# A self-attention's row maxima passed on by halves of a group's queries in place of whole groups

## The reference

```
q = q.reshape(B, NUM_KV, GROUPS, N, HEAD_DIM); k, v: [B, NUM_KV, N, HEAD_DIM]
scores = jnp.einsum('bghnd,bhsd->bghns', q, k)
attn = jax.nn.softmax(scores / SCALE, axis=-1)
out = jnp.einsum('bghns,bhsd->bghnd', attn, v)
```

## Time and profile before

| | |
|---|---|
| three runs, median (range) | 1895.57 us (1892.76 to 1900.6) |
| the profiled execution, its time | 1891.45 us |
| its span, from the first to the last instruction | 1889.7 us |
| PE busy | 1787.9 us (95%) |
| DVE busy | 1266.1 us (67%) |
| ACT busy | 1036.9 us (55%) |
| POOL busy | 363.0 us (19%) |
| maxima of pass A, L497 | 1024 times, mean 684 ns |
| exponentials of pass B, L528 | 512 times, mean 1025 ns |

### The profile page before, as it was taken

One profiled execution on the slowest core, in us unless ns is written; L12 is line 12 of the kernel. 1 busy time (PEld: TensorE's weight loads), 2 busy tenths in 40 slices (PEclk: granted clock), 3 DMA queues, 4 the chain that ended last, 5 costly groups with the idle time before them and its releaser, 6 DMA issues. The chain is left out here.

```text
span 1889.7 us, 36142 instructions
## 1 busy us (share of the span) xinstructions
PE 1787.9 (95%) x12036; PEld 1187.4 (63%) x12037; DVE 1266.1 (67%) x2510; ACT 1036.9 (55%) x2238; POOL 363.0 (19%) x403
## 2 busy tenths in 40 slices
PE   6889999999999999988989999997899999999998
PEld 3443333333333333366978899996698888888887
DVE  6588999999999999133248899994757322222323
ACT  2305878888887888921228888885226333333332
POOL 3000000000000000040004222221030444555440
PEclk9956999999999999988899999998999999999999
DMA  5601122111112210045210212111615233333333
GB/s 181 185 10 27 29 39 39 31 28 28 28 28 39 39 30 3 3 119 161 93 54 16 87 32 85 32 31 62 215 58 163 50 50 50 50 50 51 52 56 126
DMA packets 95151, 118.63 MB, mean 63 GB/s; under 512 B 18844, under 2 KB 76624, under 8 KB 93968
## 3 DMA queue, kind: packets, MB, share of 16 engines
q1 hardware_dynamic: 80016, 97.56, 18.7%
q0 software_dynamic: 13920, 19.15, 6.4%
q10 hardware_dynamic: 1104, 0.43, 0.1%
HBM read 70.37 MB, written 41.48 MB: 59 GB/s over the span
## 5 line engine op out<-in xcount | busy, mean ns | idle before, releaser
L497 DVE TENSOR_REDUCE half_max<-psA 128x1 f32<-128x512 f32 x1024 | 634.3, 684 | 36.8 <-PE psA L547 36.4
L528 ACT ACTIVATE PT<-psB 128x1024 f32<-128x1024 f32 x512 | 517.6, 1025 | 164.7 <-PE psB L557 164.5
L547 PE MATMUL psA<-KS,QS 48*128 48x512 f32 x1024 | 407.1, 481 | 23.4 <-PEq L102 14.0
L557 PE MATMUL psB<-QS,KS 50*128 50x512 f32 x1024 | 364.0, 458 | 0.4 <-ACT PT L528 0.4
L576 PE MATMUL psO<-PT,VG 128*32 128x256 f32 x4096 | 329.3, 394 | 4.7 <-ACT OU L518 0.8
L547 PEld LDWEIGHTS psA<-KS,QS 48*128 48x128 f32 x1024 | 168.9, 195 | 247.6 <-DVE half_max L497 188.9
L1866 DVE TENSOR_TENSOR m_silu<-m_psU,m_silu 128x512 f32<-128x512 f32 x104 | 71.8, 691 | 216.4 <-PE m_psU L1694 216.4
L576 PEld LDWEIGHTS psO<-PT,VG 128*32 128x32 f32 x4096 | 82.2, 108 | 191.0 <-issue 120.8
L1347 ACT ACTIVATE x_probs<-x_scores,x_neg_max 128x77 f32<-128x77 f32 x512 | 176.3, 358 | 2.9 <-DVE x_neg_max L1253 2.8
L557 PEld LDWEIGHTS psB<-QS,KS 50*128 50x128 f32 x1024 | 145.1, 187 | 19.9 <-ACT PT L528 17.4
L1197 PE MATMUL psYx<-VO,x_ET 128*128 (+1 forms) x640 | 146.0, 383 | 1.4 <-ACT x_ET L1370 0.9
(11 more groups left out here) (208 smaller groups left out, 2737.7 us busy)
## 6 DMA issues: line engine op xcount, KB each, us to landing
QS<-q_parts SPq DMA_DIRECT2D x96, 128.0 KB
q_parts<-part SPq DMA_DIRECT2D x16, 512.0 KB, 2.7
OT<-OU SPq DMA_DIRECT2D x32, 256.0 KB, 2.6
KS<-k_parts SPq DMA_DIRECT2D x32, 128.0 KB
xf_rows<-XF SPq DMA_DIRECT2D x32, 128.0 KB, 1.7
acc<-X SPq DMA_DIRECT2D x32, 128.0 KB, 1.8
m_x<-xf_rows SPq DMA_DIRECT2D x32, 128.0 KB, 2.1
WG<-in_Wg SPq DMA_DIRECT2D x8, 512.0 KB, 4.1
```

Source lines behind the costliest of these rows:

```text
L497: dve.tensor_reduce(half_max[:, h * TB + t, n:n + 1], psA[:, bank_of(slot, 2 * v + r), :], axis=AX.X, op=ALU.max).then_inc(max_taken, 1)
L528: act.activation(PT[:, k % 4, 2 * a:2 * a + 2, :].rearrange("p h n -> p (h n)"), psB[:, u % 2, :, :].rearrange("p a n -> p (a n)"), ACT.Ex ...
L547: pe.matmul(psA[:, bank_of(slot, m), :], QS[top:top + KQ, slot, h // 2, t * P:(t + 1) * P], KS[top:top + KQ, slot, n * HALF:(n + 1) * HALF ...
L557: mm = pe.matmul(psB[:, u % 2, r, :], KS[top:top + KM, slot, c * P:(c + 1) * P], QS[top:top + KM, slot, a, half * HALF:(half + 1) * HALF], ...
```

## The change

The maxima are handled by halves of a group's queries: 16 steps of pass A are one half. half_max, neg_max, max_parts and max_parts_t are half as wide. VectorE reduces and negates after 16 steps (now L509) and turns five steps into the next half; GpSimd splits twice a group. Both parts of a half now stand in one block of 32 columns, so one store carries them, where a group had two. SyncE does two trips a group, each of one store and two loads of half the row length, before it issues the load of group i+2. TensorE waits for the rows of the first half at step 0 of pass B and for those of the second at step 16; the semaphores rows_set are by half, no longer by even and odd groups. Pass A runs 16 + 10 = 26 steps ahead. The semaphores' counts change with that. The diff, cut:

```diff
@@ -369,10 +369,10 @@
-        half_max = sb("half_max", [P, NU, 2])
-        neg_max = sb("neg_max", [P, NU])
-        max_parts = sb("max_parts", [P, 2, NU], F32R)
-        max_parts_t = sb("max_parts_t", [P, 2, NU])
+        half_max = sb("half_max", [P, NC, 2])
+        neg_max = sb("neg_max", [P, NC])
+        max_parts = sb("max_parts", [P, 2, NC], F32R)
+        max_parts_t = sb("max_parts_t", [P, 2 * NC])
...
-        rows_set = [sem("rows_set_even"), sem("rows_set_odd")]
+        rows_set = [sem("rows_set_first"), sem("rows_set_second")]
...
-            def rows(i, slot):
-
-                sp.wait_ge(mt_done, count(i, 1, 1))
-                for part in range(2):
-                    sp.dma_start(m_parts[i, part, :].rearrange("(u k n) -> k u n", k=4, n=32),
-                                 max_parts_t[:, part, :]).then_inc(m_stored, 16)
-
-                sp.wait_ge(m_stored, count(i, 32, 32))
+            def rows(i, slot, half):
+
+                sp.wait_ge(mt_done, 2 * i + half + 1)
+                sp.dma_start(m_parts[i, half, :].rearrange("(u k n) -> k u n", k=4, n=32), max_parts_t[:, :]).then_inc(m_stored, 16)
+
+                sp.wait_ge(m_stored, 16 * (2 * i + half + 1))
                 for r in range(2):
-                    sp.dma_start(QS.bitcast(F32)[r * ROWS + KQ:r * ROWS + KM, slot, :, :],
-                                 m_parts[i, :, :].rearrange("j (a r n) -> r j a n", r=2, n=S)[r]).then_inc(rows_set[slot % 2], 16)
+                    sp.dma_start(QS.bitcast(F32)[r * ROWS + KQ:r * ROWS + KM, slot, :, half * HALF:(half + 1) * HALF],
+                                 m_parts[i, half, :].rearrange("(j a r n) -> r j a n", j=2, r=2, n=HALF)[r]).then_inc(rows_set[half], 16)
 
             for i in range(NG):
-                rows(i, i % SLOTS)
+                for half in range(2):
+                    rows(i, i % SLOTS, half)
                 if i + 2 < NG:
                     load(i + 2, (i + 2) % SLOTS)
-            for e in range(2):
-                sp.wait_ge(rows_set[e], NROWS * (NG // 2))
+            for half in range(2):
+                sp.wait_ge(rows_set[half], NROWS * NG)
...
-            def maxima(i):
-                pool.wait_ge(v_copied, count(i, 1, 1))
-                pool.wait_ge(neg_done, count(i, 1, 1))
-                if not (isinstance(i, int) and i < 1):
-
-                    pool.wait_ge(mt_done, count(i, 1, 0))
+            def maxima(g):
+                pool.wait_ge(v_copied, g // 2 + 1)
+                pool.wait_ge(neg_done, g + 1)
+                if g:
+
+                    pool.wait_ge(mt_done, g)
                     pool.sem_inc(T["waited_pool"], 1)
                 pool.tensor_copy(max_parts[:, 0, :], neg_max[:, :]).then_inc(m1_done, 1)
-                pool.wait_ge(m1_done, count(i, 1, 1))
+                pool.wait_ge(m1_done, g + 1)
                 pool.tensor_tensor(max_parts[:, 1, :], neg_max[:, :], max_parts[:, 0, :], ALU.subtract).then_inc(m2_done, 1)
-                pool.wait_ge(m2_done, count(i, 1, 1))
+                pool.wait_ge(m2_done, g + 1)
 
             for i in range(NG):
                 values(i, i % 2)
-                maxima(i)
+                for half in range(2):
+                    maxima(2 * i + half)
...
-            def turn_parts(i):
-
-                dve.wait_ge(m2_done, count(i, 1, 1))
-                if not (isinstance(i, int) and i < 1):
-
-                    dve.wait_ge(m_stored, count(i, 32, 0))
-                dve.transpose(max_parts_t[:, :, :], max_parts.bitcast(F32)[:, :, :]).then_inc(mt_done, 1)
-
-            def maxima(i, slot):
-                if not (isinstance(i, int) and i < 1):
-
-                    dve.wait_ge(neg_done, count(i, 1, 0))
-                for v in range(NU):
+            def turn_parts(g):
+
+                dve.wait_ge(m2_done, g + 1)
+                if g:
+
+                    dve.wait_ge(m_stored, 16 * g)
+                dve.transpose(max_parts_t[:, :], max_parts.bitcast(F32)[:, :, :].rearrange("p j u -> p (j u)")).then_inc(mt_done, 1)
+
+            def maxima(i, slot, half):
+
+                g = 2 * i + half
+                if g:
+
+                    dve.wait_ge(neg_done, g)
+                for v in range(half * NC, (half + 1) * NC):
                     for r in range(2):
                         h, t, n = unit_a(v, r)
                         dve.wait_ge(a_done, count(i, 2 * NU, 2 * v + r + 1))
-                        dve.tensor_reduce(half_max[:, h * TB + t, n:n + 1], psA[:, bank_of(slot, 2 * v + r), :],
+                        dve.tensor_reduce(half_max[:, h * (TB // 2) + t % (TB // 2), n:n + 1], psA[:, bank_of(slot, 2 * v + r), :],
                                           axis=AX.X, op=ALU.max).then_inc(max_taken, 1)
-                    if v == TURN_AT and not (isinstance(i, int) and i < 1):
-
-                        turn_parts(count(i, 1, -1))
-
-                dve.wait_ge(max_taken, count(i, 2 * NU, 2 * NU))
-                if not (isinstance(i, int) and i < 1):
-
-                    dve.wait_ge(m2_done, count(i, 1, 0))
+                    if v == half * NC + TURN_AT and g:
+
+                        turn_parts(g - 1)
+
+                dve.wait_ge(max_taken, count(i, 2 * NU, 2 * NC * (half + 1)))
+                if g:
+
+                    dve.wait_ge(m2_done, g)
                 dve.tensor_reduce(neg_max[:, :], half_max[:, :, :], axis=AX.X, op=ALU.max, negate=True).then_inc(neg_done, 1)
 
             for i in range(NG):
-                maxima(i, i % SLOTS)
-            turn_parts(NG - 1)
+                for half in range(2):
+                    maxima(i, i % SLOTS, half)
+            turn_parts(2 * NG - 1)
...
-                pe.wait_ge(rows_set[e], count(i - e, NROWS // 2, NROWS))
                 for u in range(NU):
-                    ahead = 1 if u < NU - LEAD else 2
-                    has_a = not isinstance(i, int) or i + ahead < NG
-                    if u == NU - LEAD and has_a:
-
-                        pe.wait_ge(loaded[e], count(i - e, NLOAD // 2, 2 * NLOAD))
+                    if u % NC == 0:
+                        pe.wait_ge(rows_set[u // NC], NROWS * (i + 1))
+                    ahead = 0 if u < NU - NC - LEAD else 1
+                    has_a = i + ahead < NG
+                    if u == NU - NC - LEAD and has_a:
+
+                        pe.wait_ge(loaded[1 - e], NLOAD * ((i + 1) // 2 + 1))
                     for r in range(2):
                         if has_a:
-                            pass_a(i + ahead, (slot + ahead) % SLOTS, (u + LEAD) % NU, r)
+                            pass_a(i + ahead, (slot + ahead) % SLOTS, (u + NC + LEAD) % NU, r)
                         pass_b(i, slot, u, 1 - r, r == 0)
 
                     if u >= LAG:
                         times_values(i, e, u - LAG)
-                    elif not (isinstance(i, int) and i < 1):
+                    elif i:
                         times_values(i - 1, 1 - e, u - LAG + NU)
 
             pe.wait_ge(loaded[0], NLOAD)
-            for v in range(NU):
+            for v in range(NC + LEAD):
                 for r in range(2):
                     pass_a(0, 0, v, r)
-            pe.wait_ge(loaded[1], NLOAD)
-            for v in range(LEAD):
-                for r in range(2):
-                    pass_a(1, 1, v, r)
             for i in range(NG):
                 group(i, i % SLOTS)
             for u in range(NU, NU + LAG):
...
-        T["m_parts"] = dram("m_parts", [NG, 2, GH * S], F32)
+        T["m_parts"] = dram("m_parts", [NG, 2, 2 * GH * HALF], F32)
```

## The result

The changed kernel takes 1872.78 us, the median of four runs (1866.78 to 1878.54), against 1895.69 us for the kernel before: a ratio of 0.9876, 95% interval 0.9842 to 0.9910. The forecast was 1873.7 us. The profiled execution took 1867.76 us, its span 1866.0.

What follows compares the result with a forecast made beforehand. VectorE and TensorE were nearly always busy in the full-clock common loop, with single-pass ends outside it. Start -19.8, loop +20.3, drain -16.6, boundaries -5.8 make -21.9 us: 1895.57 to 1873.7 us, range 1865 to 1886.

Steps and rivals of the forecast that it cites:

- the clock: Common loop's half-clock stretch stays 19.5 us, so it cancels; rival, rise at another distance: 1868.6 to 1881.8 us, chance 0.12.
- the start: Before pass B: it begins after 26 steps of pass A, not 42, with a shorter first trip; -19.8 us.
- the boundaries: Full-clock loop: 29 boundaries where 14 were, each trip 0.58 us shorter; 2.9 us where 8.7 were, -5.8 us.
- The loop and the drain: Common loop runs one more half, +20.3 us; pass B's drain at the end one half less, -16.6 us.
- The first rival: Trip of the maxima gets no shorter, 29 waits of 0.46 us stay: 1886.4 us, chance 0.09.
- VectorE's new work: 16 more negated maxima and turns, covered: 0 us; rival, VectorE late at every half: +7.6 us, 1881.3, chance 0.07.
- The waits for VectorE: TensorE's three waits in the common loop, 1.2 us, put down to the slots' wrap every four groups; they stay.
- The load in the way of the next trip: SyncE's group load delays the next first-half trip: a loss from 1.6 us each, up to 1962 us; chance 0.04.
- The chances: Whole kernel against a bound of 1886.1 us: 0.87 faster, 0.09 within, 0.04 slower.
- the tenth: Part of the forecast, clock and late-VectorE cases said not to lie under 1886.1 us.

Runs made afterwards that it cites:

- the last run: Changed kernel with LEAD 9 in place of 10 (pass A 25 steps ahead), rows due one step sooner: 1892.75 us, ratio 0.9990 to the kernel before.

## Why the prediction was right

The forecast was 1.0 us above the measured median, and so close by luck: the mechanism held and each part came within 1.5 us, but for the clock, which the sum let cancel. The stretch of the attention lost 27.5 us in place of 21.9: 3.5 more by the clock, 0.6 more at the start, 1.5 more at the boundaries. Ahead of it and behind it 3.8 us went the other way, and the median of the four executions lies between two near 1867 and two near 1878 us.

**The start** was forecast at -19.8 us and came to -20.4: 16 steps at VectorE's pace, as the earlier trace rows gave it, and the whole first wait of 1.07 us, of which I had given the trip 0.58. The halves with 42 steps ahead put it back (50.9 us), which shows that the lead did it.

**The loop and the drain**, +20.3 and -16.6, were measured by the copies of psO: one more half of 20.29, and 47.8 to 31.2 us. That a step outside the common loop is paid for twice, once at each end, and comes back once inside it, is what made 16 steps worth 15.5 us by the sum and 15.7 by the run with 42 steps ahead.

**The boundaries** were forecast at -5.8 and measured at -7.3 (8.7 before, 1.4 now, 29 where 14 were). The mechanism was right and the size a little low, since one term was too small. I let the trip shrink by the one store's issue alone, 0.58 us, and so left waits at two boundaries in 13. The shorter lead showed a trip 1.2 us shorter: 0.58 from the store and 0.62 from the rows, which have half the length. All trips say the same. By the semaphores' updates in the traces, the rows have landed 3.29 us behind their loads' issue in the kernel before (the median of 16 trips, from 3.08 to 3.44) and 2.76 in the changed one (of 32, from 2.63 to 3.06), and a whole trip, from the store's issue to the rows' landing, takes 5.88 and 4.77 (medians). So the two waits above 0.58 went as well, and putting the second store back left one wait, of 0.3 us. The Trainium skill (DMA: Bandwidth & Descriptors, "Anatomy of one DMA — SWDGE (gpsimd) path"), which describes another issuing path than SyncE's, has a fixed part that does not shrink with the size beside a part that goes with it. For these loads the traces show that the second part was not small: a pair of 16 KB took 3.34 us and a pair of 8 KB 2.72 (the earlier trace rows and the last run), and the measurement decides. The first rival, a trip that gets no shorter, is refuted by the profile after, which has no wait for the rows, and by the same runs.

**VectorE's new work** was put at nothing, under a margin of 0.6 us a half. It cost nothing: the halves stayed at 20.28. But the margin left is 0.16 us, by the run with two more maxima, and the run with the turn at once suggests that it also hangs on where in the half the work stands. The 0.6 was wrong because I had summed the maxima at the pace of the start, 0.599 us each, and compared with the half's length. In the common loop VectorE is busy 527.51 of 535 us, so it stands idle for 0.28 us a half (7.5 us over 26.4 halves), and some of that cannot be used: in the run with two more maxima it still waits 0.16 us for TensorE, 1.8 us behind a copy of psO (300.99, the copy at 299.15). The work itself was put too high as well, at up to 0.51 us a half: the negated maxima delay the next maximum by 0.23.

**The waits for VectorE**, three of 1.2 us, stayed as three of 1.3, in the old and the new order alike; that the slots' wrap makes them was argued from the banks and from their distance of four groups, and not tested by itself.

**The clock** I took to behave as before, 19.5 us of common work at 0.50. In the profiled execution it was 11.2, worth about 3.5 us, and 5.1 us were lost ahead of the attention in the same execution, so the sum looks closer than its parts. Over the five profiles with pass A 25 or 26 steps ahead and no idle matmuls the rise stood 9, 11, 24, 24 and 28 us behind the first step of pass B, 19 on average. The assumption holds on average, over few runs and in kernels that differ, and for no single execution.

**The load in the way of the next trip**, the slower rival, did not come: the halves do not alternate between long and short, and the longest trip in the changed kernel, 5.50 us to the rows' landing, delayed no matmul.

**The chances.** The 0.87 for faster does not take off the tenth that its own sentence names; with it, it is 0.78.

## What to carry to other kernels

Where two passes share a loop and one runs ahead, each step of lead is paid at the start by the one engine and at the end by the other; price it by the two ends and subtract the loop's own step. What bounds the lead is a round trip with a due time: measure its slack by making it due one step sooner and reading the waits, since a trip that is covered shows nothing. A cover that comes from summing an engine's work was an upper bound here (0.6 us, and 0.16 real); adding work until it shows gives the real one.

## What was not expected

After its fall ahead of the attention the granted clock stayed at 0.50 while TensorE was busy for all of 38 us with pass A and the matmuls whose result is not used, and in every run it rose only in the common work: 9.1 us behind the first step of pass B in the repeat of the changed kernel, 30.6 us in the run with the turn at once. What sets this distance stays open. In the 42 further executions of the kernel before, the time goes with the mean clock, from 1905.9 us at 0.950 to 1889 at 0.961, some 1.6 us for each 0.001 of the clock; that is most of the spread which any comparison here has to live with.

Pairs of loads of two partitions landed 0.5 to 0.6 us sooner, a sixth to a fifth of their time, with 8 KB each in place of 16 KB; the forecast had given the smaller size nothing.
